# A graph layer on one core: one-hot rows from TensorE products and a relu, and one product per tile in place of two

## The chip, the core and the metric

The kernel runs on one core of one Trainium2 chip. The metric is the device time of one execution in microseconds (us). Times are given as the median of several executions; the profile is of one execution, whose own time is given beside its span.

## What is computed

A layer of a graph network in float32, over N = 6250 nodes with C = 96 features and E = 100,000 edges. Edges are sorted by their target node `dst`. With `BN` for "subtract the mean over all rows, divide by the root of the variance plus 1e-5, scale and shift":

```python
h = relu(layernorm(x))                                   # 6250 x 96
node_feat = BN(relu(h @ W_node + b_node))                # 6250 x 96
edge_feat = BN(relu(edge_attr @ W_edge + b_edge))        # 100000 x 96, edge_attr is 100000 x 4
message = concat([h[src], h[dst], edge_feat], axis=1)    # 100000 x 288
message = BN(relu(message @ W_msg + b_msg))              # 100000 x 96
agg = segment_sum(message, dst, N)                       # 6250 x 96
out = x + agg + node_feat
```

## The kernel before

The message product is split: `h @ W_msg[:96]` and `h @ W_msg[96:192]` are made once for each node and stored in DRAM as `p_table` and `q_table`; the third part acts on the edge features. So a message is relu(p[src] + q[dst] + edge part).

Edges are worked in tiles of 128 and groups of four tiles (512 edges); there are 196 groups, and the last has two tiles. The five engines run programs written by hand, each in its own order, and meet through semaphores. The parts in order of time:

- **Head.** SP loads the nodes; VectorE and ScalarE make the layer norm, TensorE turns the rows and makes `p_table`. POOL at the same time gathers source rows for the first 12 groups directly from `x`. VectorE splits the edge attributes in three bfloat16 parts (`take_off`, L884), SP stores them as 30 rows `x_stack` in DRAM, and VectorE makes from `dst` the place of each edge in its group's window of 96 nodes (`dst_rel`, L907 to L915), with a check that all edges of a group fall in that window (`flag`).
- **Statistics stage.** For all 196 groups TensorE makes relu(edge part), and VectorE takes its mean and variance (L691, L567, L936). The first 12 groups' own rows of `p` are made here too.
- **Message loop** (from L981 on VectorE, `passes(...)` on each engine; `BODY` = 4 groups in one pass of the loop, 49 passes). For each group: SP loads 30 rows of `x_stack` for two groups at once (L423), reads the number of the group's first node (L427) and loads the 96 rows of `q_table` from there (`q_win`, L428). POOL gathers 4 × 128 rows of `p_table` by source node into a ring of 60 groups (L455); it waits only for a free slot. TensorE makes the edge product (L737), turns the bfloat16 one-hots (`hot_b`, L743), adds edge part and `q` part of each tile in PSUM (L759, L761), and sums the messages to the window's nodes with a float32 one-hot (`hot`, L772). ScalarE copies the results of L737 and L743 to SBUF (L605, L607), makes the relu of the messages (L618) and their squares (L622). VectorE builds both one-hots by comparing `dst_rel` with a ramp (L994, L997), adds the gathered rows (L1008), adds messages and squares to `acc` for the mean and variance (L1015), and adds the window to `agg` (L1024).
- **End.** TensorE sums `acc` over the partitions (L813), VectorE makes scale and shift, and twelve blocks of 512 nodes and a rest go through a product with the scale (L825), an addition (L1089) and a store (L441).

The buffers of the loop are two or four groups deep, and the orders overlap: TensorE works at `edges(g + 2)`, `products(g + 1)`, `window_sum(g)`; SP runs up to three groups ahead of `products`. If the check in `flag` fails, a slow general path runs in place of the loop; with these inputs it does not.

```python
wait(sp, pre_summed, g - 3)
base = sp.value_load(base_b[0:1, bass.ds(g, 1)], min_val=0, max_val=N - 1)
sp.dma_start(q_win[0:WIN, j, :], q_table[bass.ds(base, WIN), :]).then_inc(q_in[j], 16)
```

`value_load` reads a number from SBUF into a register of the engine's sequencer and checks its range.

Of the kernel before, what the change touches and what calls it, by code (L numbers as in the profile page):

```python
# [17 lines left out]
N, E, C, EF = 6250, 100000, 96, 4  # L18
P = 128
TILE = P  # L20
# [15 lines left out]
KROWS = len(STACK) * EROWS  # L36
SPLIT_F = EROWS * EP // P
# [18 lines left out]
PACKED = VEC_AT + 7  # L56
# [8 lines left out]
MW = C + 1 + C  # L65


W_GATHER, W_SUMS, W_SCALES, W_DIAG = (8, 4), 5, 9, 2


def graph_layer(nc, x_rows, x_nodes, x_t, src_cols, dst_cols, group_base, edge_rows, packed, w_edge, out_t):
# [5 lines left out]
    x_stack = nc.dram_tensor("x_stack", (KROWS, EP), bf16, kind="Internal").ap()  # L77

    with ExitStack() as ctx:
# [3 lines left out]
        def sem(name):  # L83
# [20 lines left out]
        dst_rel = sb("dst_rel", [P, NG, TPG])  # L104
        base_b = sb("base_b", [P, NG], i32)
        hot = sb("hot", [P, 4, TPG, WIN])
        dst_i = hot[:, :, :, :].bitcast(i32).rearrange("p a t w -> p (a t w)")
        dst_i2 = hot[:, 2:4, :, :].bitcast(i32).rearrange("p a t w -> p (a t w)")
        r_sb = sb("r_sb", [P, 2, 2 * GROUP])
        hot_n = sb("hot_n", [P, 2, GROUP])  # L110
        msg = sb("msg", [P, 2, TPG, MW])
        acc = sb("acc", [P, TPG, MW])
# [6 lines left out]
        hot_b = ln_buf[:, :, :].rearrange("p a f -> p (a f)")[:, 0:2 * TPG * WIN].bitcast(bf16).rearrange(  # L119
            "p (a t w) -> p a t w", a=4, w=WIN)  # L120
        ident_b = sb("ident_b", [P, P], bf16)
        q_win = sb("q_win", [P, 4, C])
# [6 lines left out]
        w3c = sb("w3c", [P, C])  # L129
        we5 = sb("we5", [EROWS, M1])  # L130
        we_split = sb("we_split", [EROWS, 3, M1], bf16)
        we_stack = sb("we_stack", [P, M1], bf16)
        sc = sb("sc", [C, 16])
        t_col = sb("t_col", [C, M1])
        fold = sb("fold", [C, M1])
        s_diag = sb("s_diag", [M1, C])
        bad = sb("bad", [P, 4])
# [7 lines left out]
        pb_b = pb[:, :, :].bitcast(bf16)  # L145
# [13 lines left out]
        rows_cleared = sem("rows_cleared")  # L159
# [44 lines left out]
        turn_built = sem("turn_built")  # L204
        hot_built = sem("hot_built")
        hot_turned = sem("hot_turned")
        hot_kept = sem("hot_kept")
# [19 lines left out]
        gen_square = sem("gen_square")  # L227
# [5 lines left out]
        sums_made = sem("sums_made")  # L233
# [116 lines left out]
        def _(sp):  # L350
# [795 lines left out]
```

## Time and profile before

| | |
|---|---|
| time, median of 3 runs | 1090.58 us (1089.98 to 1091.89) |
| time of the profiled execution | 1093.96 us |
| its span, first to last instruction | 1092.2 us |
| mean granted TensorE clock | 0.889 |
| head, to the first edge product of the statistics stage | 70.5 us |
| first edge product of the message loop | 240.9 us |
| first and last start of a gather from `p_table` | 72.6 and 1068.0 us |

The profile's page gives the busy time of the engines, the span in 40 slices, the chain of work that ended last, the costliest groups of instructions, and the DMAs. Other views give the same by stage, in order of time, or by who waited for whom. PE is TensorE's matmuls, PEld its weight loads, DVE VectorE, ACT ScalarE, POOL GpSimd, SP the engine that only issues DMAs here; L12 is line 12 of the kernel. A float32 matmul shows as two records. A granted clock of 1.00 is 2.4 GHz, and 0.50 is 1.2 GHz.

### The profile page before, as it was taken

Reading aid. Unit: us, or ns where it says so; the run is one execution under the profiler, and the core shown is the slowest. Engines: PE = TensorE matmul, PEld = TensorE weight load, DVE = VectorE, ACT = ScalarE, POOL = GpSimd, SP = SyncE. Lnnn points to the kernel's source line nnn. Section 1 sums busy time; section 2 is a strip of 40 time slices with the busy share of each in tenths; the row PEclk is TensorE's granted clock in tenths of the full one; section 3 lists DMA queues with packets and bytes.
Section 4 is the critical chain, followed back from the end, with each engine's and each line's share of the span. In section 5 each row is a group of like instructions: output and inputs, shape, how many; then the busy total and the mean of one; then the engine's idle time right before and its main releaser. Section 6 shows DMA issues by size and latency. Waiting matters only on the chain.

```text
span 1092.2 us, 23979 instructions
## 1 busy us (share of the span) xinstructions
PE 839.5 (77%) x6383; PEld 726.1 (66%) x6385; DVE 724.6 (66%) x1579; ACT 542.9 (50%) x1012; POOL 826.6 (76%) x786
## 2 busy tenths in 40 slices
PE   2537866639999999999777777777777776877777
PEld 2425622229999999999666666667667666766663
DVE  8678799978898898988444454444444444444445
ACT  3735988836666666666333333333333333333330
POOL 6877777777777777777777777777777777777771
PEclk9867988869999999999888888887898887888889
DMA  8665333352222222222222222222222222222223
GB/s 278 184 225 135 75 85 89 86 150 60 61 57 65 60 58 63 61 59 62 54 49 53 51 52 50 55 49 50 49 56 49 51 54 50 53 49 53 51 45 96
DMA packets 79842, 82.82 MB, mean 76 GB/s; under 512 B 52322, under 2 KB 57074, under 8 KB 79690
## 3 DMA queue, kind: packets, MB, share of 16 engines
q0 software_dynamic: 25024, 38.49, 16.6%
q1 hardware_dynamic: 54148, 42.83, 14.0%
q10 hardware_dynamic: 646, 1.25, 0.4%
q14 instruction: 17, 0.14, 0.0%
q8 instruction: 7, 0.11, 0.0%
HBM read 65.84 MB, written 13.34 MB: 72 GB/s over the span
## 4 chain that ended last, share of the span: by engine, by line
PE 31%; POOL 28%; issue 16%; DMA 11%; DVE 6%; ACT 5%; ACTq 0%; SPq 0%; DVEq 0%; POOLq 0%
POOL ring L455 28%; DMA ring<-p_table,src_idx 8%; PE pc L759 8%; PE pc L761 8%; PE pd L772 6%; DVE edge_st L936 4%; ACT r_sb L567 3%; DMA big_a<-acc 3%; PE pc L666 2%; PE pb L743 2%; PE pa L737 2%; PE pa L691 1%; DVE ln_buf L857 1%; ACT ring L515 1%; DVE ring L878 1%
## 5 line engine op out<-in xcount | busy, mean ns | idle before, releaser
L455 POOL DMA_INDIRECT ring<-p_table,src_idx x734 | 772.9, 1053 | 223.8 <-issue 199.7
L759 PE MATMUL pc<-w3c,r_sb 128*128 128x96 f32 x1564 | 334.0, 298 | 6.3 <-issue 5.9
L761 PE MATMUL pc<-q_win,hot_n 128*128 128x96 f32 x1564 | 322.7, 290 | 0.0
L1008 DVE TENSOR_TENSOR pc<-pc,ring 128x384 f32<-128x384 f32 x196 | 110.8, 565 | 315.3 <-POOLq L482 286.4
L618 ACT ACTIVATE msg<-pc 128x384 f32<-128x384 f32 x196 | 96.4, 492 | 438.3 <-DVE pc L1008 435.5
L772 PE MATMUL pd<-hot,msg 128*97 128x96 f32 x1564 | 192.2, 271 | 136.7 <-ACT msg L618 133.8
L759 PEld LDWEIGHTS pc<-w3c,r_sb 128*128 128x128 f32 x1564 | 262.5, 211 | 13.3 <-issue 10.7
L772 PEld LDWEIGHTS pd<-hot,msg 128*97 128x97 f32 x1564 | 165.8, 181 | 153.7 <-ACT msg L618 111.1
L761 PEld LDWEIGHTS pc<-q_win,hot_n 128*128 128x128 f32 x1564 | 258.6, 208 | 0.0
L1015 DVE TENSOR_TENSOR acc<-acc,msg 128x772 f32<-128x772 f32 x196 | 186.1, 950 | 0.0
L936 DVE BATCH_NORM_STATS2 edge_st<-r_sb 96x512 f32 (+1 forms) x196 | 121.2, 674 | 17.3 <-ACT r_sb L567 15.9
L605 ACT ACTIVATE r_sb<-pa 97x512 f32<-97x512 f32 x196 | 113.3, 578 | 6.4 <-PE pa L737 6.4
L994 DVE TENSOR_TENSOR ln_buf<-dst_rel,pk 128x384 bf16<-128x384 f32 x196 | 108.3, 552 | 5.2 <-issue 5.0
L607 ACT CAST hot_n<-pb 96x512 f32<-96x512 bf16 x196 | 111.4, 569 | 0.3 <-PE pb L743 0.3
L997 DVE TENSOR_TENSOR hot<-dst_rel,pk 128x384 f32<-128x384 f32 x196 | 107.5, 549 | 0.0
L622 ACT ACTIVATE msg<-msg 128x384 f32<-128x384 f32 x196 | 103.2, 526 | 6.2
L743 PEld LDWEIGHTS pb<-ident_b,ln_buf 128*96 128x96 bf16 x782 | 77.5, 140 | 28.1 <-DVE ln_buf L994 8.7
L743 PE MATMUL pb<-ident_b,ln_buf 128*96 128x128 bf16 x782 | 87.6, 242 | 0.3 <-DVE ln_buf L994 0.3
L737 PE MATMUL pa<-xs,we_stack 128*97 128x512 bf16 x196 | 84.5, 431 | 3.9 <-DMA xs<-x_stack 3.9
L455 POOL DMA_INDIRECT ring<-in_x_rows,src_idx x48 | 53.5, 1114 | 18.4 <-issue 14.3
L691 PE MATMUL pa<-xs,we_stack 128*97 128x512 bf16 x98 | 36.0, 455 | 37.9 <-DMA we_stack<-we_split 23.2
L567 ACT ACTIVATE r_sb<-pa 96x1024 f32<-96x1024 f32 x49 | 50.0, 1020 | 16.9 <-DVE edge_st L936 8.4
(110 smaller groups left out, 545.7 us busy)
## 6 DMA issues: line engine op xcount, KB each, us to landing
xs<-x_stack SPq DMA_DIRECT2D x196, 60.0 KB, 1.8
ring<-p_table,src_idx POOLq DMA_INDIRECT x734
q_win<-q_table SPq DMA_DIRECT2D x196, 36.0 KB
x_stack<-ring SPq DMA_DIRECT2D x6, 980.0 KB
ring<-in_x_nodes SPq DMA_DIRECT2D x5, 480.0 KB, 9.8
big_a<-acc SPq DMA_DIRECT2D x1, 2400.0 KB, 12.9
p_table<-ring SPq DMA_DIRECT2D x12, 192.0 KB, 2.5
q_table<-ring SPq DMA_DIRECT2D x12, 192.0 KB
```

The source lines that it names most:

```text
L455: nc.gpsimd.indirect_dma_start(out=ring[:, tile * C:(tile + 1) * C], out_offset=None, in_=table, in_offset=bass.IndirectOffsetOnAxis(ap=id ...
L605: nc.scalar.activation(r_sb[0:M1, j % 2, 0:n], pa[0:M1, j % 2, 0:n], ACT.Relu).then_inc(edge_relu, 1)
L607: nc.scalar.copy(hot_n[0:WIN, j % 2, 0:n], pb_b[0:WIN, j % 2, 0:n]).then_inc(hot_kept, 1)
L743: last = nc.tensor.transpose(pb_b[0:WIN, j % 2, t * TILE:(t + 1) * TILE], hot_b[:, j, t, :], ident_b[:, :])
L759: nc.tensor.matmul(out, r_sb[:, j % 2, t * TILE:(t + 1) * TILE], w3c[:, :], start=True, stop=False)
L761: last = nc.tensor.matmul(out, hot_n[:, j % 2, t * TILE:(t + 1) * TILE], q_win[:, j, :], start=False, stop=True)
L772: last = nc.tensor.matmul(pd[0:M1, j % 2, 0:WIN], msg[:, j % 2, t, 0:M1], hot[:, j, t, :], start=(t == 0), stop=(t == n - 1))
L936: last = V.bn_stats(edge_st[:, bass.ds(u * 2 + half, 1), :].rearrange("c a s -> c (a s)"), r_sb[0:C, k % 2, half * GROUP:half * GROUP + n])
L994: V.tensor_tensor(hot_b[:, j, 0:n, :], rel, ramp[:, :].unsqueeze(1).to_broadcast([P, n, WIN]), ALU.is_equal).then_inc(turn_built, 1)
L997: V.tensor_tensor(hot[:, j, 0:n, :], rel, ramp[:, :].unsqueeze(1).to_broadcast([P, n, WIN]), ALU.is_equal).then_inc(hot_built, 1)
L1008: V.tensor_tensor(pc[:, j % 2, 0:n], pc[:, j % 2, 0:n], ring[:, bass.ds((g % RING) * (TPG * C), n)], ALU.add).then_inc(pre_added, 1)
L1015: V.tensor_tensor(acc[:, 0:n, :], acc[:, 0:n, :], msg[:, j % 2, 0:n, :], ALU.add).then_inc(acc_added, 1)
```

## The change

**One-hots.** In the head, the places of the edges are made in rows (98 × 1024, one number for each edge) rather than columns: relative to the first node of the edge's tile, and relative to that of its group. Each is stored as r, and r² in two bfloat16 parts; these six rows are appended to `x_stack`, which has now 36 rows. With w for a node of the window, 1 − (r − w)² = (1 − w²) + 2wr − r² is linear in (1, r, r²), so a product with fixed coefficients makes it, and its relu is the one-hot. The coefficients for the tile (30 nodes, `TWIN`) are 30 more columns of `we_stack`; those for the group (96 nodes) are `hot_coef`.

**One product for a tile.** The edge product now gives 128 rows: 96 of edge features, one of ones, and 30 of the tile's one-hot; one relu on ScalarE makes them all (`r_sb`). Its partner `w3q` holds the edge weights, the bias, and 30 rows of `q_table`. So L759 and L761 become one product, and SP loads 30 rows for each tile in place of 96 for each group. The group's one-hot is made by four small products into PSUM and a relu on VectorE into `hm`.

**Sums.** `hm` holds for each tile the one-hot, the messages and a column of ones. The window product has 193 columns in place of 96 and gives also messages-times-messages (`gram`); its last column is the sums, its diagonal the sums of squares. The squares on ScalarE, the `acc` addition and the products L813 go. The check is now on windows of 30 nodes for tiles and 96 for groups.

```diff
             sp.wait_ge(stack_stored, 16 * len(STACK))
-            sp.wait_ge(rows_cleared, 1)
+            sp.wait_ge(rel_ready, 1)
+            for k in range(6):
+                sp.dma_start(x_stack[KROWS + k:KROWS + k + 1, :].rearrange("r (p f) -> p (r f)", p=ROWS),
+                             rel_out[:, k, :]).then_inc(rel_stored, 16)
...
+            sp.wait_ge(rel_stored, 16 * 6)
+            sp.wait_ge(main_ready, 1)
             sp.wait_ge(flag_ready, 1)
...
-                            wait(sp, edge_lin, g - 2)
-                            sp.dma_start(xs[0:KROWS, j // 2, :], x_stack[:, bass.ds(g * GROUP, 2 * GROUP)]).then_inc(
+                            wait(sp, hot_lin, g - 2)
+                            sp.dma_start(xs[0:KX, j // 2, :], x_stack[:, bass.ds(g * GROUP, 2 * GROUP)]).then_inc(
                                 x_main[j // 2], 16)
                         wait(sp, pre_summed, g - 3)
-                        base = sp.value_load(base_b[0:1, bass.ds(g, 1)], min_val=0, max_val=N - 1)
-                        sp.dma_start(q_win[0:WIN, j, :], q_table[bass.ds(base, WIN), :]).then_inc(q_in[j], 16)
+                        _, at_node = nc.values_load_multi_w_load_instructions(
+                            bases[0:1, bass.ds(g * TPG + NG, TPG)], [mybir.EngineType.SP], min_val=0, max_val=N - 1)
+                        for t in range(tiles(i, j)):
+                            sp.dma_start(w3q[M1:M1 + TWIN, j, t, :], q_table[bass.ds(at_node[t], TWIN), :]).then_inc(
+                                q_in[j], 16)
...
-                    nc.scalar.activation(r_sb[0:M1, j % 2, 0:n], pa[0:M1, j % 2, 0:n], ACT.Relu).then_inc(edge_relu, 1)
-                    act.wait_ge(hot_turned, g + 1)
-                    nc.scalar.copy(hot_n[0:WIN, j % 2, 0:n], pb_b[0:WIN, j % 2, 0:n]).then_inc(hot_kept, 1)
+                    nc.scalar.activation(r_sb[:, j % 2, 0:n], pa[:, j % 2, 0:n], ACT.Relu).then_inc(edge_relu, 1)
...
-                    wait(act, win_summed, g - 1)
-                    wait(act, acc_added, g - 1)
+                    wait(act, win_summed, g - 3)
...
-                    nc.scalar.square(msg[:, j % 2, 0:n, M1:MW], msg[:, j % 2, 0:n, 0:C]).then_inc(msg_square, 1)
...
-                        last = nc.tensor.transpose(pb_b[0:WIN, j % 2, t * TILE:(t + 1) * TILE], hot_b[:, j, t, :],
-                                                   ident_b[:, :])
+                        at_edge = j % 2 * GROUP + t * TILE
+                        last = nc.tensor.matmul(pb[:, j % 2, t * WIN:(t + 1) * WIN],
+                                                xs[:, j // 2, at_edge:at_edge + TILE], hot_coef[:, :],
+                                                start=True, stop=True)
...
-                    pe.wait_ge(q_in[j], i * 16 + 16)
+                    pe.wait_ge(q_in[j], i * (16 * TPG) + 16 * n)
...
-                        nc.tensor.matmul(out, r_sb[:, j % 2, t * TILE:(t + 1) * TILE], w3c[:, :],
-                                         start=True, stop=False)
-                        last = nc.tensor.matmul(out, hot_n[:, j % 2, t * TILE:(t + 1) * TILE], q_win[:, j, :],
-                                                start=False, stop=True)
+                        last = nc.tensor.matmul(pc[:, j % 2, t * C:(t + 1) * C], r_sb[:, j % 2, t * TILE:(t + 1) * TILE],
+                                                w3q[:, j, t, :], start=True, stop=True)
...
-                        last = nc.tensor.matmul(pd[0:M1, j % 2, 0:WIN], msg[:, j % 2, t, 0:M1], hot[:, j, t, :],
+                        last = nc.tensor.matmul(pd[0:M1, j % 2, 0:HW], hm[:, j, t, WIN:HW], hm[:, j, t, :],
...
-                    V.tensor_tensor(hot_b[:, j, 0:n, :], rel, ramp[:, :].unsqueeze(1).to_broadcast([P, n, WIN]),
-                                    ALU.is_equal).then_inc(turn_built, 1)
-                    V.tensor_tensor(hot[:, j, 0:n, :], rel, ramp[:, :].unsqueeze(1).to_broadcast([P, n, WIN]),
-                                    ALU.is_equal).then_inc(hot_built, 1)
+                    V.tensor_scalar(hm[:, j, 0:n, 0:WIN], pb[:, j % 2, 0:n * WIN].rearrange("p (t w) -> p t w", w=WIN),
+                                    0.0, None, ALU.max).then_inc(hot_built, 1)
...
-                    V.tensor_tensor(acc[:, 0:n, :], acc[:, 0:n, :], msg[:, j % 2, 0:n, :],
-                                    ALU.add).then_inc(acc_added, 1)
+                    V.tensor_tensor(gram[:, :], gram[:, :], pd[0:M1, j % 2, WIN:HW], ALU.add).then_inc(gram_added, 1)
...
-            V.tensor_tensor(w3c[C:M1, :], pd[C:M1, 0, 0:C], bm_row[C:M1, :], ALU.add).then_inc(main_ready, 1)
+            V.tensor_tensor(w3q[C:M1, :, :, :].rearrange("p j t c -> p (j t) c"),
+                            pd[C:M1, 0, 0:C].unsqueeze(1).to_broadcast([1, BODY * TPG, C]),
+                            bm_row[C:M1, :].unsqueeze(1).to_broadcast([1, BODY * TPG, C]),
+                            ALU.add).then_inc(main_ready, 1)
...
-            link(V.tensor_scalar(sc[:, 0:2], pd[0:C, 0, 0:2], 1.0 / E, None, ALU.mult))
+            link(V.tensor_tensor(diag[:, :], gram[0:C, 0:C], ident[0:C, 0:C], ALU.mult))
+            link(V.tensor_reduce(sc[:, 1:2], diag[:, :], AX, ALU.add))
+            V.tensor_scalar(sc[:, 0:1], gram[0:C, C:M1], 1.0 / E, None, ALU.mult)
+            link(V.tensor_scalar(sc[:, 1:2], sc[:, 1:2], 1.0 / E, None, ALU.mult))
```

The order of SP's instructions for one group in the message loop. Before (`ISA` is a register instruction of the sequencer, the first with the wait, the next two the range check, the last the DMA's address):

```order
L427 ISA [waits pre_summed]
L427 TENSOR_LOAD base_b
L427 ISA x2
L428 ISA
L428 DMA q_win<-q_table 96x96
```

With the change:

```order
L435 ISA [waits pre_summed]
L435 TENSOR_LOAD bases
L435 ISA x8
L438 ISA
L438 DMA w3q<-q_table 30x96
L438 ISA
L438 DMA w3q<-q_table 30x96
L438 ISA
L438 DMA w3q<-q_table 30x96
L438 ISA
L438 DMA w3q<-q_table 30x96
```

One load now fills four registers, four range checks follow it, and four DMAs stand where one stood.

VectorE in the head, between the split of the edge weights and the second subtraction of `take_off`. Before:

```order
L901 CAST we_split<-we 5x97 [waits dve_step]
L907 TENSOR_TENSOR dst_rel<-hot,base_b 128x784 [waits dst_in]
L911 TENSOR_SCALAR msg<-dst_rel 128x784 [waits dve_step]
L912 TENSOR_TENSOR msg<-msg 128x784 [waits dve_step]
L913 TENSOR_REDUCE bad<-msg 128x1 [waits dve_step]
L914 COPY bad<-msg 32x1
L915 TENSOR_SCALAR bad<-bad 128x2 [waits dve_step]
L917 MEMSET msg 128x4 x2
L919 MEMSET r_sb 128x2048
L920 MEMSET hot_n 128x1024
L922 TENSOR_REDUCE flag<-pd 1x1 [waits bad_counted]
L884 TENSOR_TENSOR big_b<-big_b,ring 128x3920 [waits split_step]
```

With the change (the ten rows from L908 to L921 stand there twice, once for tiles and once for groups):

```order
L908 TENSOR_TENSOR r_sb<-w3q,row_base 98x1024 [waits dst_in]
L912 CAST hm<-r_sb 98x1024 [waits dve_step]
L913 TENSOR_TENSOR r_sb<-r_sb 98x1024
L914 CAST hm<-r_sb 98x1024 [waits dve_step]
L915 TENSOR_TENSOR hm<-r_sb,hm 98x1024 [waits dve_step]
L917 TENSOR_SCALAR r_sb<-r_sb 98x1024 [waits dve_step]
L918 TENSOR_TENSOR r_sb<-r_sb 98x1024 [waits dve_step]
L919 TENSOR_REDUCE bad<-r_sb 98x1 [waits dve_step]
L920 TENSOR_REDUCE bad<-r_sb 97x1
L921 TENSOR_SCALAR bad<-bad 128x2 [waits dve_step]
```

The subtraction of `take_off` stands behind all of them, with one memset of `w3q` (128x1536) between.

## Rows read from the trace of the kernel before

**Rows 1.** The page, parts 1 and 2, and waits: engine, line waited for: us, times, longest
```profile
PE 839.5 (77%) x6383; PEld 726.1 (66%) x6385; DVE 724.6 (66%) x1579; ACT 542.9 (50%) x1012; POOL 826.6 (76%) x786
...
GB/s 278 184 225 135 75 85 89 86 150 60 61 57 65 60 58 63 61 59 62 54 49 53 51 52 50 55 49 50 49 56 49 51 54 50 53 49 53 51 45 96
...
DVE pc L1008 <- POOLq L482: 286.4, 100, 5.2
```

**Rows 2.** Busy time by stage, us: all engines, granted clock, DMA share, GB/s
```profile
72.60:226.00 153.40, 110.43 (x483) 60.31 (x482) 138.03 (x288) 120.21 (x161) 116.01 (x123) 0.87 0.38 94
255.00:505.00 250.00, 250.00 (x2469) 242.11 (x2468) 225.29 (x448) 167.60 (x341) 198.20 (x170) 1.00 0.27 61
520.00:1060.00 540.00, 401.45 (x2913) 360.80 (x2911) 261.33 (x530) 198.67 (x404) 417.74 (x402) 0.85 0.23 51
```

**Rows 3.** The line of the gathers: ns min/median/max, first and last start
```profile
L455 POOL DMA_INDIRECT ring<-p_table,src_idx x734: 940/944/1510, 72.6 to 1068.0; - x184
```

**Rows 4.** The gathers alone by the same stages: POOL busy (count), clock, DMA, GB/s
```profile
72.60:226.00 153.40, 116.01 (x123) 0.87 0.38 94
255.00:505.00 250.00, 198.20 (x170) 1.00 0.27 61
520.00:1060.00 540.00, 417.74 (x402) 0.85 0.23 51
```

**Rows 5.** Timeline from 702 us, POOL and VectorE: start us, us, engine line operation
```profile
702.38 0.94 POOL L455 DMA_INDIRECT ring<-p_table,src_idx  x1 [0.30 <-issue]
702.71 0.57 DVE L1008 TENSOR_TENSOR pc<-pc,ring 128x384 f32<-128x384 f32 x1 [2.84 <-POOLq L482]
703.19 0.95 DVE L1015 TENSOR_TENSOR acc<-acc,msg 128x772 f32<-128x772 f32 x1
703.63 1.32 POOL L455 DMA_INDIRECT ring<-p_table,src_idx  x1 [0.30 <-issue]
```

**Rows 6.** Timeline from 300 us, TensorE's weight loads in one group
```profile
300.13 0.13 PEld L737 LDWEIGHTS pa<-xs,we_stack 128*97 128x97 bf16 x1
...
301.04 0.30 PEld L759 LDWEIGHTS pc<-w3c,r_sb 128*128 128x128 f32 x2
...
301.27 0.30 PEld L761 LDWEIGHTS pc<-q_win,hot_n 128*128 128x128 f32 x2
...
302.38 0.77 PEld L772 LDWEIGHTS pd<-hot,msg 128*97 128x97 f32 x8
...
303.07 0.13 PEld L737 LDWEIGHTS pa<-xs,we_stack 128*97 128x97 bf16 x1
```

**Rows 7.** Waits of SP's queue
```profile
SPq L427 <- PE pc L761: 409.7, 192, 6.4
```

**Rows 8.** Lines 427, 428 and 423 on SP: ns min/median/max, first and last start
```profile
L427 SPq FUSED_REGOPS  x384: 37/152/161, 232.2 to 1047.9; - x192
L427 SPq TENSOR_LOAD <-base_b x196: 268/428/1922, 230.2 to 1047.6; - x196
L427 SPq SEQ_ASSERT  x196: 18/18/18, 232.4 to 1048.1; - x196
...
L428 SPq FUSED_REGOPS  x196: 37/37/48, 232.4 to 1048.2; - x196
L428 SPq MOVE q_win<-q_table x196: 29/29/45, 232.5 to 1048.2; - x196
L428 SPq DMA_DIRECT2D q_win<-q_table x196: 317/317/902, 232.6 to 1048.3; - x196
...
L423 SPq DMA_DIRECT2D xs<-x_stack x98: 373/373/2358, 229.0 to 1038.8; - x98
L423 SPq FUSED_REGOPS  x94: 42/50/51, 243.0 to 1018.0; - x94
```

**Rows 9.** Timeline, SP from 255 us
```profile
256.43 0.32 SPq L428 DMA_DIRECT2D q_win<-q_table  x1
256.93 0.32 SPq L410 DMA_DIRECT2D res<-in_x_t  x1
```

**Rows 10.** Timeline of the head, VectorE
```profile
42.26 0.95 DVE L907 TENSOR_TENSOR dst_rel<-hot,base_b 128x784 f32<-128x784 int32 x1
43.24 0.57 DVE L911 TENSOR_SCALAR msg<-dst_rel 128x784 f32<-128x784 f32 x1
43.85 0.98 DVE L912 TENSOR_TENSOR msg<-msg 128x784 f32<-128x784 f32 x1
...
49.22 0.08 DVE L922 TENSOR_REDUCE flag<-pd 1x1 int32<-1x2 f32 x1
50.98 4.24 DVE L884 TENSOR_TENSOR big_b<-big_b,ring 128x3920 f32<-128x3920 f32 x1 [1.68 <-ACT ring L515]
```

**Rows 11.** Timeline before the message loop, SP and VectorE
```profile
229.01 1.15 SPq L423 DMA_DIRECT2D xs<-x_stack  x1
...
240.23 0.26 DVE L971 TENSOR_TENSOR w3c<-pd,pk 1x96 f32<-1x96 f32 x1 [3.63 <-DMA big_a<-acc]
```

**Rows 12.** Timeline of the end, VectorE
```profile
1075.17 0.15 DVE L1072 TENSOR_SCALAR sc<-pd 96x2 f32<-96x2 f32 x1 [1.35 <-PE pd L813]
```

More of the change, by code:

```diff
@@ L690, in p1_unit @@
                 for half in range(2):
-                    last = nc.tensor.matmul((pa, pb)[k % 2][0:M1, half, :], we_stack[:, :],
+                    last = nc.tensor.matmul((pa, pb)[k % 2][0:M1, half, :], we_stack[:, 0:M1],
                                             xs[:, k, half * GROUP:(half + 1) * GROUP], start=True, stop=True)
@@ L839, in _ @@
             V = nc.vector
[L841 removed]
+            V.memset(zeros[:, :], 0.0).then_inc(zeroed, 1)
             V.memset(ones[:, :], 1.0)
@@ L845, in _ @@
             V.memset(xs[:, :, :], 0.0)
-            V.memset(w3c[:, :], 0.0)
-            V.memset(q_win[:, :, :], 0.0)
+            V.memset(hot_coef[:, :], 0.0)
+            V.memset(gram[:, :], 0.0)
+            V.memset(hot_n[:, :, :], 0.0)
             V.memset(bad[:, :], 0.0)
@@ L911, in _ @@
-            link(V.tensor_scalar(far, rel, -(WIN - 1) / 2.0, None, ALU.add))
-            link(V.tensor_tensor(far, far, far, ALU.mult))
-            V.tensor_reduce(bad[:, 0:1], far[:, 0:full], AX, ALU.max)
-            link(V.tensor_copy(bad[0:LAST_ROWS, 1:2], far[0:LAST_ROWS, full:full + 1]))
-            V.tensor_scalar(bad[:, 2:4], bad[:, 0:2], (WIN / 2.0) ** 2, None, ALU.is_gt).then_inc(bad_ready, 1)
-            for k in range(2):
-                V.memset(msg[:, k, :, C:M1], 1.0)
-            V.memset(r_sb[:, :, :], 0.0)
@@ L921, in _ @@
+            last.then_inc(bad_ready, 1)
+            dve.sem_inc(rel_ready, 1)
+            V.memset(w3q[:, :, :, :], 0.0)
             dve.wait_ge(bad_counted, 1)
-            V.tensor_reduce(flag[0:1, 0:1], pd[0:1, 0, 0:2], AX, ALU.max).then_inc(flag_ready, 1)
+            V.tensor_reduce(flag[0:1, 0:1], pd[0:1, 0, 0:4], AX, ALU.max).then_inc(flag_ready, 1)
             take_off(1)
@@ L1025, in add_sums @@
                                     ALU.add).then_inc(win_added, 1)
-                for j in range(3):
+                for j in range(2):
                     build_hot(0, j)
@@ L1120 @@
         packed[:C, VEC_AT + k] = w[name]
+    for at, rel, n in ((HOT_AT, REL_T, TWIN), (HOT_AT + TWIN, REL_G, WIN)):
+        w_at = _np.arange(n)
+        low = (1 - w_at * w_at) % 64
+        packed[0, at:at + n] = 1 - w_at * w_at - low
+        packed[EROWS, at:at + n] = low
+        packed[rel, at:at + n] = 2 * w_at
+        packed[rel + 1:rel + 3, at:at + n] = -1.0
     w_edge = _np.zeros((EROWS, M1), _np.float32)
```

198 lines of the change are left out of this document (105 added, 93 removed).

## Prediction

> **What bounds the kernel now.** I read the page's busy shares, then the gathers by stage, then the waits. The reader should see in [rows 1] that no engine is full over the whole span, that POOL's indirect gathers are the costliest group and that VectorE waits 286.4 us for POOL's `gathered` counts. The stages in [rows 2] differ: from 255 to 505 us TensorE is busy all of the time at its 2.4 GHz level (granted clock 1.00) and works off the backlog of gathered groups; from 520 to 1060 us it is busy 74% at 0.85 and waits. POOL never stops: its gathers run from 72.6 to 1068.0 us [rows 3], and the queue behind them is what ends last. So today's end is 734 gathers long, and what SP, TensorE and VectorE need for a group of four gathers is hidden as long as it keeps the mean below (1068 − 241) / 196 = 4.2 us [rows 3, 11]. That number decides this case.
>
> **The gathers get faster.** In [rows 4] a gather takes 943 ns busy in 123 cases while the statistics stage runs (VectorE is 90% busy there too, on one-input work), 1,166 ns while the message loop runs at full speed, and 1,039 ns in the last stage; with the 0.30 us between two of them [rows 5] the periods are 1.25, 1.47 and 1.34 us. [rows 5] show the cause: the gather that starts at 702.38 takes 0.94 us beside L1008, which reads PSUM and SBUF; the one at 703.63 takes 1.32 us beside L1015, 0.95 us with both inputs in SBUF. The change takes L1015 away and both L994 and L997 (two SBUF inputs, 0.55 us each), and puts in their place a relu from PSUM and an addition with one PSUM input. What is left with two SBUF inputs in the loop is L978, once in four groups. So the gathers go to 1.24 us: 734 × 1.24 = 910 us in place of 995, from about 75.5 us (3 us later, for the two-input passes in the head, below). POOL would then issue its last gather at 986, and with the 24.2 us from the last gather to the end [rows 3] (1,092.2 − 1,068.0), less 1 us (below), the span would be 1,009 us. That is the floor.
> The Trainium skill (SBUF — State Buffer, Who interferes with whom) says that a Vector instruction with two SBUF inputs contends only with GpSimd work that reads SBUF, and it infers that descriptor generation is not such work. By that rule the gathers would stay where they are and the floor would be 1,092 us; [rows 4, 5] speak against it.
>
> **TensorE, VectorE and ScalarE.** In the full stage TensorE needs 2.94 us for a group, from one L737 at 300.13 to the next at 303.07 [rows 6]. Of these, 16 f32 product records take 0.11 us each (0.23 from 301.04 to 301.27 for two), and the change drops the 8 of L761; four small transposes become four small products. The window product goes from 96 to 193 columns: its 8 records take 0.69 us, 302.38 to 303.07, and twice the columns is at most twice that, so +0.7 against −0.9 us. So about 2.8 us, some 3.2 at a granted clock of 0.85: below SP's number, so priced at nothing. VectorE loses 0.55 + 0.55 + 0.95 us and gains some 0.55 + 0.25; ScalarE loses L607 and L622. Both were covered and stay so.
>
> **SP, the part that I think decides.** Today SP issues one DMA of 96 rows for a group and then waits: 409.7 us for products in all [rows 7]. The change makes it load four numbers, check each, and issue four DMAs of 30 rows, and the products of a group wait for all four. The register rows [rows 8] and two DMAs that start back to back, 256.43 and 256.93 [rows 9], give the price: 0.50 us = 0.317 + 0.037 + 0.029 and three gaps of 0.04. For a group, when SP waits for nothing:
> - wait and address, 0.05 + 0.04 = 0.09;
> - the load, 0.27 to 0.43 for one number, mean 0.35, + 0.04 = 0.39;
> - four pairs of check and assert, 4 × (0.152 + 0.018 + 0.08) = 1.00;
> - four DMAs at 0.50 = 2.01;
> - half an `xs` load, (0.050 + 0.029 + 0.373 + 0.12) / 2 = 0.29; a quarter of a `res` load, 0.13; counters and branches, some 0.1.
> That is 4.0 us before the load of four numbers is priced. No row shows such a load: it costs nothing more at the least, and three more loads, 3 × 0.27 = 0.81, at the most. I take 0.35, nearer to one instruction than to four, since one address is computed. The check is also uncertain: its 0.152 stands beside 0.037 to 0.05 for other register rows of two or three operations. If the 0.11 difference is a wait for the loaded number, only the first check pays it, and the group is 0.33 cheaper. So SP's pace is 3.7 at the least, 4.8 at the most; 4.35 is my value.
>
> **The head.** L907 to L915 (42.26 to 46.1) and the memsets behind them, up to 49.22, go [rows 10]. In their place VectorE makes 2 × 10 passes, most over 98 × 1024: by [rows 10] a two-input pass of 784 takes 0.95 to 0.98 us, so 1.23 for 1024; a one-input pass 0.57, so 0.72. Twice (four at 1.23, three at 0.72, one reduction at 1.2, a third of one, a small one) is 18.4 us, plus 1.4 for the memset of `w3q` (three quarters of the 2048 columns that are cleared today). The subtraction L884 that follows then starts at 62.5 in place of 50.98: +11.5 us, and it is on the path, since `we_stack` and the last `x_stack` piece come behind it. SP then puts six stores of 0.2 MB on its queue before the first `xs` load; at the 185 to 225 GB/s of the head [rows 1] that is 5 to 6 us, some 4 of it not covered. The statistics stage and what follows move by 15 us. POOL doesn't feel it: it needs the flag at 72.6 [rows 3], and the flag moves from 49.22 [rows 10] to about 62.
> Before the loop, L971 becomes 1 × 1536 in place of 1 × 96 (+1.4 us), and SP, which today fills its buffers from 229.01 on [rows 11], now waits for it. SP enters the loop at 240.23 + 15 + 1.7 + 0.6 = 257.5 us.
>
> **The sum.** 257.5 + 196 × 4.35 (852.6) = 1,110. The last window lands 2 us later (as the `xs` loads do), the last group's products, addition, relu and window product take 2, and from L1072 at 1075.17 to the end it is 17.0 us today [rows 12]. Ahead of it the sums L813 and the wait for them give way to the addition to `gram` and four small VectorE steps, 1.5 us together, where today 2.4 pass. Span 1,110 + 4 + 1.5 + 17.0 = 1,132.5; today's is 1,092.2, so +40.3. The profiled execution took 1,093.96 in all, 3.4 above the median 1,090.58; the forecast in the median's terms is 1,131.
>
> **The rivals.**
> 1. *SP is cheaper than I price it* (checks 0.33 less, the four-number load free). Pace 3.7 to 4.1: 257.5 + 196 × 3.85 + 22.5 = 1,035 span, with the gathers' floor at 1,009 just below. This is **faster**, and it decides as soon as SP's pace is under 4.14 us, where 257.5 + 196 × pace + 22.5 is today's span. For it: the register rows of other kinds are short. Against: every check in the rows took 0.152. Chance 0.26, 1,008 to 1,083.
> 2. *Each number pays for its own load.* The group takes 4.0 + 0.81 = 4.8 us, the span 257.5 + 941 + 22.5 = 1,221. For it: even one number takes 0.27 to 0.43, far more than any other register row. The Trainium skill (Runtime: NRT & Kernel Launch) puts such loads at about 200 ns for each register even in bulk; by that estimate the pace is 4.6 and the span 1,182. No row here shows it. Chance 0.25, 1,170 to 1,240.
> 3. *TensorE falls to its 1.2 GHz level* because it waits for SP between short bursts. At half the clock 2.8 us become 5.6 and the span 257 + 1,098 + 23 = 1,378. Against: at 74% busy the clock was 0.85 [rows 2]. Chance 0.03.
> 4. *The gathers don't get faster*, and SP is cheap: the end stays with POOL, about 1,092 to 1,095. Chance 0.03.
> My case, a pace of 4.2 to 4.6 with SP ahead of all, has 0.39 and its own range is 1,103 to 1,180; 0.04 is left for a pace that lands on today's time.
>
> **How the numbers follow.** A run can tell about 0.2% from nothing. Faster: rival 1 and a little of rival 4, 0.28. Same: 0.04. Slower: 0.68. The range must take in rival 1's middle and most of rival 2: 1,018 to 1,215 leaves out the bottom of rival 1 (0.05), the top of rival 2 (0.08) and rival 3.
>
> **What would show it.** Right: SP's own waits for products nearly vanish from 409.7 us; the starts of the last `w3q` DMA of two groups lie 4.2 to 4.6 us apart throughout; TensorE waits for DMAs into `w3q`; POOL's gathers take 0.94 us in every stage and end near 990, long before the span; no two stages of the loop differ, as 255 to 505 and 520 to 1060 do now. Wrong: SP still waits and VectorE waits for POOL to the end (rival 1 at its floor), gathers still at 1.04 us or more (rival 4), or TensorE full at a clock near 0.5 (rival 3). The first loop instruction should start near 258 us, the first edge statistics near 87 in place of 72.75.

## The result, and the profile after

The changed kernel takes 1,120.8 us, the kernel before 1,090.8 on the same chip (medians of four executions each): the ratio is 1.026, 95% interval 1.024 to 1.029. The change makes the kernel **2.6% slower**. The forecast was 1,131 with a range of 1,018 to 1,215. Of the changed kernel's four executions three took 1,117.4 to 1,121.5 us; the fourth took 1,359.9 with a mean granted clock of 1.00 where the others had 0.87, is left out of the ratio, and is not explained. The profiled execution took 1,120.07 us, its span is 1,118.3.

The page of the changed kernel: busy time, and the shares of the chain that ended last, by engine and by line.
```profile
PE 781.5 (70%) x4800; PEld 635.8 (57%) x4800; DVE 544.2 (49%) x1401; ACT 369.7 (33%) x620; POOL 750.8 (67%) x786
...
SPq 54%; issue 21%; DVE 10%; PE 7%; ACT 5%; DMA 3%; ACTq 0%; DVEq 0%
SPq L438 28%; SPq L435 20%; DVE edge_st L941 4%; SPq L431 3%; ACT r_sb L577 3%; SPq L416 2%; PE pc L670 2%; DMA big_a<-zeros 1%; DMA xs<-x_stack 1%; PE pa L695 1%; PE pc L762 1%; PE pd L773 1%; DVE ln_buf L856 1%; DVE ring L877 1%; SPq L273
```
Against [rows 1] every compute engine has less to do, and more than half of the chain is now SP's queue: L438 issues the `w3q` loads, L435 waits, loads the four numbers and checks them.

The gathers, their line and then alone by stage (columns as in [rows 3, 4]; the last gather starts at 991.7, inside the third stage).
```profile
L466 POOL DMA_INDIRECT ring<-p_table,src_idx x734: 940/944/1500, 75.6 to 991.7; - x184
```
```profile
72.60:226.00 153.40, 115.92 (x124) 0.85 0.40 100
255.00:505.00 250.00, 189.03 (x201) 0.88 0.29 62
520.00:1060.00 540.00, 357.33 (x379) 0.88 0.26 57
```
The gathers run at 0.94 us in all stages, where [rows 4] had 1.17 and 1.04 in the loop. They end 76 us earlier than in [rows 3], and yet the span is 26 us longer. TensorE is no longer full in the first part of the loop: 185.16 us busy from 255 to 505 us, in the view of all engines, where [rows 2] have 250.00.

SP's lines: ns min/median/max, first and last start.
```profile
L435 SPq FUSED_REGOPS  x972: 66/147/162, 254.3 to 1091.3; - x195
L435 SPq SEQ_ASSERT  x784: 18/18/24, 254.5 to 1091.5; - x196
L435 SPq TENSOR_LOAD <-bases x196: 458/464/557, 253.7 to 1089.9; - x196
...
L438 SPq FUSED_REGOPS  x782: 37/42/48, 255.3 to 1092.1; - x196
L438 SPq MOVE w3q<-q_table x782: 29/29/42, 255.4 to 1092.2; - x196
L438 SPq DMA_DIRECT2D w3q<-q_table x782: 327/328/1177, 255.5 to 1092.3; - x196
```
196 loads lie between 253.7 and 1,089.9 us, 4.29 us from one to the next. SP's queue has no wait at all between 260 and 1,100 us; its last one of note stands ahead of the loop, and TensorE waits instead. From the waits of SP's queue, then of all engines (engine, line waited for: us, times, longest):
```profile
SPq L421 <- DVE w3q L979: 15.9, 1, 15.9
```
```profile
PE pa L741 <- DMA xs<-x_stack: 204.1, 91, 8.2
```
The 409.7 us for products of [rows 7] are gone, and so are the 286.4 us of VectorE for POOL [rows 1].

### The profile page after: what moved, and what is told of

Read it like the earlier page. It is cut to its first block, busy times and chain, and to the rows that moved or that the text cites. A ratio compares the mean times of both kernels' runs of the same rounds, so it can differ in the third digit from the quotient of the medians.

```text
span 1118.3 us, 22745 instructions
## 1 busy us (share of the span) xinstructions
PE 781.5 (70%) x4800; PEld 635.8 (57%) x4800; DVE 544.2 (49%) x1401; ACT 369.7 (33%) x620; POOL 750.8 (67%) x786
## 4 chain that ended last, share of the span: by engine, by line
SPq 54%; issue 21%; DVE 10%; PE 7%; ACT 5%; DMA 3%; ACTq 0%; DVEq 0%
SPq L438 28%; SPq L435 20%; DVE edge_st L941 4%; SPq L431 3%; ACT r_sb L577 3%; SPq L416 2%; PE pc L670 2%; DMA big_a<-zeros 1%; DMA xs<-x_stack 1%; PE pa L695 1%; PE pc L762 1%; PE pd L773 1%; DVE ln_buf L856 1%; DVE ring L877 1%; SPq L273 1%
## 5 line engine op out<-in xcount | busy, mean ns | idle before, releaser
L466 POOL DMA_INDIRECT ring<-p_table,src_idx x734 | 693.5, 945 | 223.8 <-issue 197.6
L773 PE MATMUL pd<-hm 128*97 128x193 f32 x1564 | 341.4, 368 | 0.0
L773 PEld LDWEIGHTS pd<-hm 128*97 128x97 f32 x1564 | 281.0, 191 | 9.8
L762 PE MATMUL pc<-w3q,r_sb 128*128 128x96 f32 x1564 | 245.7, 307 | 13.9 <-DMA w3q<-q_table 7.7
L762 PEld LDWEIGHTS pc<-w3q,r_sb 128*128 128x128 f32 x1564 | 218.2, 216 | 20.3 <-issue 9.7
L741 PE MATMUL pa<-xs,we_stack 128*128 128x512 bf16 x196 | 83.4, 426 | 204.3 <-DMA xs<-x_stack 204.1
L615 ACT ACTIVATE r_sb<-pa 128x512 f32<-128x512 f32 x196 | 116.8, 596 | 326.6 <-PE pa L741 323.8
L1004 DVE TENSOR_SCALAR hm<-pb 128x384 f32<-128x384 f32 x196 | 109.1, 557 | 222.6 <-PE pb L747 195.5
L625 ACT ACTIVATE hm<-pc 128x384 f32<-128x384 f32 x196 | 96.3, 491 | 312.2 <-DVE pc L1015 304.2
L1015 DVE TENSOR_TENSOR pc<-pc,ring 128x384 f32<-128x384 f32 x196 | 110.8, 565 | 97.9 <-PE pc L762 91.5
L466 POOL DMA_INDIRECT ring<-in_x_rows,src_idx x48 | 57.1, 1189 | 17.8 <-issue 14.3
L695 PE MATMUL pa<-xs,we_stack 128*97 128x512 bf16 x98 | 35.4, 448 | 37.5 <-DMA we_stack<-we_split 22.5
L577 ACT ACTIVATE r_sb<-pa 96x1024 f32<-96x1024 f32 x49 | 50.0, 1020 | 18.6 <-PE pa L695 9.6
```

Of the source, the lines that this page charges most:

```text
L466: nc.gpsimd.indirect_dma_start(out=ring[:, tile * C:(tile + 1) * C], out_offset=None, in_=table, in_offset=bass.IndirectOffsetOnAxis(ap=id ...
L577: nc.scalar.activation(r_sb[0:C, k % 2, :], (pa, pb)[k % 2][0:C, :, :].rearrange("c a b -> c (a b)"), ACT.Relu).then_inc(p1_relu, 1)
L615: nc.scalar.activation(r_sb[:, j % 2, 0:n], pa[:, j % 2, 0:n], ACT.Relu).then_inc(edge_relu, 1)
L741: nc.tensor.matmul(pa[:, j % 2, 0:n * TILE], we_stack[:, :], xs[:, j // 2, j % 2 * GROUP:j % 2 * GROUP + n * TILE], start=True, stop=True) ...
L762: last = nc.tensor.matmul(pc[:, j % 2, t * C:(t + 1) * C], r_sb[:, j % 2, t * TILE:(t + 1) * TILE], w3q[:, j, t, :], start=True, stop=True)
L773: last = nc.tensor.matmul(pd[0:M1, j % 2, 0:HW], hm[:, j, t, WIN:HW], hm[:, j, t, :], start=(t == 0), stop=(t == n - 1))
```

## The experiments

The median of the kernel before was 1,093.1 to 1,094.2 us in these comparisons and 1,090.8 in the first, so a difference of 2 or 3 us between two comparisons says nothing. Two theories were set against each other: **A**, SP's own instructions set the pace; **B**, the four small DMAs themselves do.

**e1: no range checks.** The checks of the four numbers go.
```
-    bases[0:1, bass.ds(g * TPG + NG, TPG)], [mybir.EngineType.SP], min_val=0, max_val=N - 1)
+    bases[0:1, bass.ds(g * TPG + NG, TPG)], [mybir.EngineType.SP], min_val=0, max_val=N - 1,
+    skip_runtime_bounds_check_because="each is the first node of a tile, checked by flag")
```


> Theory A (SP's own instructions set the pace of the loop, 4.28 us for a group, of which the four range checks are 4 x 0.26 = 1.03 us): the pace falls to 3.25 us if nothing else holds, so the gathers set the end; last gather at 992 us as with the change, span 1,010 to 1,018 us, time near 1,015 us, SP waits for products again. Rival B (the pace is set by the DMAs themselves, their queue or their landing, not by SP's instructions): the checks cost nothing, time stays at 1,120 us.

Measured 1,018.8 us, ratio 0.932 (0.931 to 0.934). The same DMAs, loads and products, and 102 us less than the changed kernel. SP waits for products again, and VectorE for gathers (waits of SP's queue, then of all engines):
```profile
SPq L435 <- PE pc L763: 64.0, 38, 5.9
```
```profile
DVE pc L1016 <- POOLq L494: 168.3, 56, 5.6
```
A holds, and the floor is POOL's.

**e2: one more load.** A one-number load with its check is put ahead of the four-number load, and nothing uses it.
```
+    sp.value_load(bases[0:1, bass.ds(g, 1)], min_val=0, max_val=N - 1)
     _, at_node = nc.values_load_multi_w_load_instructions(
```


> One more load of one number with its check for each group, unused. Theory A: 0.3 to 0.5 us for the load, 0.26 for the check, 0.1 for the address, so +0.7 to +0.85 us for each of 196 groups: time 1,257 to 1,287 us. Rival B: 1,120 us.

Measured 1,233.5 us (two runs), ratio 1.128 (1.125 to 1.132): 113 us, or 0.58 us a group, more than the changed kernel's 1,120.8, and less than expected. The two loads, the new one first:
```profile
L435 SPq TENSOR_LOAD <-bases x196: 438/443/542, 259.4 to 1204.9; - x196
...
L436 SPq TENSOR_LOAD <-bases x196: 298/302/318, 260.2 to 1205.7; - x196
```
The load of *one* number takes 443 ns and that of *four*, right behind it, 302. So the count of numbers costs nothing that shows. What stands around the load does: in e3, below, the loads of two numbers take 0.640 us on SP and 0.663 on ScalarE (medians).

**e3: the issue split.** ScalarE's queue loads, checks and issues tiles 2 and 3 of a group, SP tiles 0 and 1; the products wait for both.
```
-    for t in range(tiles(i, j)):
+    for t in range(2):
...
+    act.dma_start(w3q[M1:M1 + TWIN, j, 2 + t, :], q_table[bass.ds(at_node[t], TWIN), :]).then_inc(q_act[j], 16)
...
-    pe.wait_ge(q_in[j], i * (16 * TPG) + 16 * n)
+    pe.wait_ge(q_in[j], i * 32 + 32)
+    pe.wait_ge(q_act[j], i * 32 + 32)
```


> ScalarE's sequencer loads, checks and issues for two of the four tiles of a group, SP for the other two. Theory A: SP needs 2.7 us for a group and ScalarE about 3.6 (1.1 us of work, 2.1 for its half, waits), both below the gathers' 5.0 us; time near 1,015 us, last gather at 992. Rival B: the number and size of DMAs are the same and they share the DMA engines: 1,120 us.

Measured 1,018.2 us, ratio 0.932 (0.930 to 0.933).

**e7: split, and no checks.**

> Both together. Theory A: the gathers already set the end of each one alone, so nothing is gained over them: 1,010 to 1,018 us. Rival B: 1,120 us. If the end is not with the gathers but with ScalarE's or SP's rest, this one is faster than either alone.

Measured 1,019.1 us, ratio 0.932 (0.930 to 0.933). Either cure alone reaches the floor, and both together win nothing more. A holds: e1 has every transfer of the changed kernel, and e3 has them too, issued from two queues.

That settles the new bound. The second question is why the gathers got faster, and what they cost the kernel before. **C**: VectorE's instructions with two inputs in SBUF stretch them. **D**: they don't.

**e4, e5, e6: the kernel before, without the addition, without the one-hots, without either.** In e5 and e6 L994 is replaced in the same way as L997 below, from the fifth group on.
```
-    V.tensor_tensor(acc[:, 0:n, :], acc[:, 0:n, :], msg[:, j % 2, 0:n, :], ALU.add).then_inc(acc_added, 1)
+    dve.sem_inc(acc_added, 1)
```
```
-    V.tensor_tensor(hot[:, j, 0:n, :], rel, ramp[:, :].unsqueeze(1).to_broadcast([P, n, WIN]),
-                    ALU.is_equal).then_inc(hot_built, 1)
+    V.memset(hot[:, j, 0, 0:1], 0.0).then_inc(hot_built, 1)
```


> The kernel before, without the addition of L1015 (VectorE, 128x512, both inputs in SBUF), so that the message sums are left out and the scale and shift that come of them are wrong. Theory C (a VectorE instruction that reads two inputs from SBUF stretches the gathers beside it; 0.385 to 0.40 us a group of the kernel before is such stretch, and the addition is the larger share of it): about 33 us less than the kernel before, near 1,060; gathers' mean between 0.97 and 0.99 us where the stage rows of the kernel before had 1.04 to 1.17. Rival D (the skill's rule: such instructions do not contend with descriptor generation; the stretch comes of something else, VectorE's general load or the transfers): no change, near 1,093, gathers' mean as before.

> The kernel before, with the one-hots of L994 and L997 built for the first four groups alone (a one-column memset in their place behind that), so that tables of other groups are used and the output is wrong by that. Theory C: about 37 us less than the kernel before, near 1,055, if both one-hot builds stretch the gathers; near 1,072 if only L997 does, since the slope of the gathers' time on the overlap with L994 is about zero in the trace of before. Rival D: no change, near 1,093, though VectorE has some 1.3 us a group less to do.

> The kernel before with both edits: neither the addition of L1015 nor the one-hot builds behind the fourth group. Message sums are left out and the one-hots are stale. Theory C: the gathers run at their floor of 1.247 us each, 734 of them, and the time is 1,018 to 1,025. Rival D: near 1,093.

(The addition is 128x772, as [rows 5] show, not 128x512 as e4's text has it.)

Measured: e4 1,039.2 us, ratio 0.951 (0.950 to 0.953); e6 1,014.9, ratio 0.929 (0.928 to 0.931). e5: 1,088.6 to 1,091.0 in seven executions and 1,054.5 in an eighth, whose mean granted clock was 0.73 where the others had 0.89. The gathers' line in the kernel before, e4, e5 and e6 (count, then busy us and mean ns of one):
```profile
L455 POOL DMA_INDIRECT ring<-p_table,src_idx x734 | 772.9, 1053 | 223.8 <-issue 199.7 <-DMA ring<-p_table,src_idx 14.0 <-DVE pc L1008 10.1
L455 POOL DMA_INDIRECT ring<-p_table,src_idx x734 | 719.1, 980 | 223.7 <-issue 197.8 <-DMA ring<-p_table,src_idx 24.1 <-DVE pc L1008 1.8
L455 POOL DMA_INDIRECT ring<-p_table,src_idx x734 | 769.2, 1048 | 223.7 <-issue 201.8 <-DMA ring<-p_table,src_idx 22.0
L455 POOL DMA_INDIRECT ring<-p_table,src_idx x734 | 693.0, 944 | 223.7 <-issue 200.5 <-DMA ring<-p_table,src_idx 20.1 <-DVE pc L1015 3.0
```
With neither, the kernel before reaches the floor, so VectorE's instructions do stretch the gathers, and D falls. But the shares are not sums of parts: without the addition 54 us go, not 33; without the one-hots 3.3 us in the seven executions, not 37; without both 78. The traces say why. Put down the time of each gather over 0.944 us to the VectorE instruction that is under way at its start: in the kernel before the addition has 70.3 us (193 gathers), L997 9.3 (71), L994 0.6 (2). In e4 L997 has 14.2 and L994 12.2 (145 gathers): with the addition gone, the one-hots lie across more starts. In e5 the addition has 76.2 (193 gathers again). The sums, 80.0, 26.2, 76.3 and 0.1 us, differ by what the times differ by, to 2 us. e5's eighth execution lies where C expected e5; it has no trace, and what e5 saves in that other rhythm stays open. The next four kernels ask what the price is of.

**e8: the addition's twin in the changed kernel.** To e3 comes, in each group, a VectorE maximum of 128x772, both inputs in SBUF, whose result nothing uses.
```
+    scratch = hot_n[:, :, :].rearrange("p a f -> p (a f)")[:, 0:772]
+    V.tensor_tensor(scratch, scratch, scratch, ALU.max).then_inc(spent, 1)
```


> The changed kernel with its issue split over two sequencers (as e3), and in each group one VectorE maximum of 128x772 more, both inputs and the output in SBUF, whose result nothing uses. VectorE has room for it (busy about half of the span). Theory C: the gathers are stretched again, mean about 0.99 us, and the time is some 30 to 40 us above e3, near 1,050. Rival D: as e3, near 1,018.

Measured 1,090.8 us (ten executions, 1,082 to 1,100), ratio 0.997 (0.994 to 0.999): 72.6 us above e3, twice what was expected, from 196 instructions of 0.95 us on an engine that is half idle. The timeline shows what happens (start us, us, engine, line, operation):
```profile
698.28 0.94 POOL L468 DMA_INDIRECT ring<-p_table,src_idx  x1 [0.30 <-issue]
699.17 0.95 DVE L1044 TENSOR_TENSOR hot_n<-hot_n 128x772 f32<-128x772 f32 x1
699.53 1.41 POOL L468 DMA_INDIRECT ring<-p_table,src_idx  x1 [0.30 <-issue]
```
The maximum starts during one gather, which still takes 0.94 us, and ends at 700.12, 0.59 us after the next has started; that one takes 1.41, or 0.47 us too long. The gather is not slowed in proportion. It is longer by what is left, at its start, of the VectorE instruction under way, less some 0.12 us.

**e9, e10, e11: one input, half the length, bfloat16.** The same place in the group, with other instructions.
```
+    V.tensor_scalar(scratch, scratch, 0.0, None, ALU.max).then_inc(spent, 1)
+    wait(dve, spent, 2 * g + 1)
+    V.tensor_scalar(scratch, scratch, 0.0, None, ALU.max).then_inc(spent, 1)
```
That is e9, with e8's 128x772 `scratch`. e10 keeps e8's line with `scratch` cut to 386 columns, and e11 with 1,544 columns of the same buffer as bfloat16.

> The control of e8: in place of the maximum of 128x772 with two inputs in SBUF, two maxima with a constant in each group, 128x772 too, each with one input and its output in SBUF, so that VectorE moves the same output twice and is busy for about as long. Theory C (it is the second SBUF input that stretches the gathers): near 1,018, gathers' mean 0.945 us as in e3. Rival E (any long VectorE instruction on SBUF stretches them): 1,060 or more, gathers' mean over 1.0 us. Rival F (e8's price came from VectorE's time in its chain and not from the gathers): between the two, with the gathers unchanged.

> As e8, with a maximum of 128x386: half the length, some 0.5 us. Theory C with a price by the length of the overlap: half of e8's 72.6 us above e3, near 1,054, or less where part of it falls into the 0.3 us between two gathers. With a price by the number of instructions: the whole, near 1,090.

> As e8, with operands in bfloat16, 128x1544: the same bytes as e8's 128x772 in fp32. The trace of before had L994, whose output is bfloat16, at no stretch, and L997, with an fp32 output, at 0.4 us per us of overlap. If the type of the output decides: near e3, 1,018. If two inputs in SBUF decide, whatever their type: 1,080 to 1,130 by how long it lasts.

Measured: e9 1,034.6 us, ratio 0.946 (0.944 to 0.947), so 16.5 above e3; e10 1,034.9, ratio 0.945 (0.944 to 0.947), 16.7 above; e11 1,096.2, ratio 1.003 (1.002 to 1.005), 78 above. e9 lies between the values expected by C and by E, and e10 far below the half. F, VectorE's own chain, falls: the gathers' time over 0.944 us is 14.3 us in e9, 16.3 in e10 and 77.6 in e8 against 1.0 in e3, so the gathers alone account for the prices. One rule explains both. In the timelines, first e10, then e9:
```profile
705.86 0.55 DVE L1044 TENSOR_TENSOR hot_n<-hot_n 128x386 f32<-128x386 f32 x1
706.25 0.97 POOL L468 DMA_INDIRECT ring<-p_table,src_idx  x1 [0.31 <-issue]
```
```profile
709.20 0.55 DVE L1044 TENSOR_SCALAR hot_n<-hot_n 128x772 f32<-128x772 f32 x1
709.48 1.09 POOL L468 DMA_INDIRECT ring<-p_table,src_idx  x1 [0.30 <-issue]
709.79 0.56 DVE L1046 TENSOR_SCALAR hot_n<-hot_n 128x772 f32<-128x772 f32 x1
```
In e10 0.16 us of the maximum are left when the gather starts, and it loses 0.03; in e9 0.27 are left and it loses 0.15. So half the length costs a quarter: in e10 95 gathers are held, by 0.15 us on average, and in e8 190 by 0.40. And an instruction with one input in SBUF and its output there holds a gather up too; it costs less here since it is over in 0.55 us and the second of the pair starts when the gather is under way. Not every such instruction does: in the statistics stage of the kernel before 107 gathers start with a batch_norm_stats (L936, one input in SBUF, an output of 6 columns) under way and 0.47 us of it left on average, and none takes over 0.95. The maximum of e9 moves its 772 columns in 0.55 us where the one with two inputs takes 0.95; whether that faster form or the wide output in SBUF makes the difference was not tried. The bfloat16 maximum of the same bytes lasts as long and costs as much, so the type isn't what counts:
```profile
702.20 0.95 DVE L1046 TENSOR_TENSOR hot_n<-hot_n 128x1544 bf16<-128x1544 bf16 x1
702.50 1.46 POOL L468 DMA_INDIRECT ring<-p_table,src_idx  x1 [0.30 <-issue]
```
The Trainium skill (SBUF — State Buffer, Who interferes with whom) has VectorE and GpSimd share a port pair as an exclusive lock, and the shape of these rows agrees with a lock. In the same section the Trainium skill infers that a two-input instruction leaves descriptor generation alone; the gathers are issued by GpSimd, and e8, e10 and e11, 72.6, 16.7 and 78 us above e3, speak against that.

**e12: the same work in another place.** If the price is of the moment, the kernel before needs no change of its work, only of its order. The addition goes ahead of L1008, right behind the wait for the gathered rows; nothing is left out (`add_msg` is the addition of the group before).
```
     dve.wait_ge(pre_summed, g + 1)
     dve.wait_ge(gathered, g + 1)
+    if before is not None:
+        add_msg(*before)
     V.tensor_tensor(pc[:, j % 2, 0:n], pc[:, j % 2, 0:n],
```


> The kernel before with two of its VectorE instructions in the other order, and nothing left out: in each group the addition of the message sums (L1015, 128x772, 0.95 us) stands right behind the wait for the gathered rows and ahead of L1008, where it stood behind L1008. In the traces a gather is longer by what is left, at its start, of a VectorE instruction on SBUF, less some 0.1 us, and a gather that has started is not longer. The addition of the kernel before started 0.7 to 0.9 us behind a gather's start, and so was in flight when the next one began, 1.25 us behind it; moved ahead it would start some 0.25 to 0.3 us behind a gather's start and be done at 1.25. Theory C in this form (the price is of the place, not of the work): 1,020 to 1,050, the gathers' mean between 0.945 and 0.985, where what is left comes of the one-hots L994 and L997. If the price is of the work (so many us of two-input instructions anywhere beside gathers): as before, near 1,093.

Measured 1,070.6 us, ratio 0.979 (0.977 to 0.981): 22.7 us faster than the kernel before by the order of two instructions, though the expected 1,020 to 1,050 was missed.
```profile
699.69 0.94 POOL L455 DMA_INDIRECT ring<-p_table,src_idx  x1 [0.30 <-issue]
699.88 0.96 DVE L1017 TENSOR_TENSOR acc<-acc,msg 128x772 f32<-128x772 f32 x1 [2.55 <-POOLq L482]
...
700.94 0.94 POOL L455 DMA_INDIRECT ring<-p_table,src_idx  x1 [0.30 <-issue]
...
701.85 0.55 DVE L997 TENSOR_TENSOR hot<-dst_rel,pk 128x384 f32<-128x384 f32 x1
...
702.19 1.03 POOL L455 DMA_INDIRECT ring<-p_table,src_idx  x1 [0.30 <-issue]
```
The addition (L1017 here) now ends at 700.84, ahead of the next start at 700.94, and costs neither gather anything, where the same instruction cost 0.38 us in [rows 5]. But the one-hots behind it were pushed across the start at 702.19, and from 255 to 505 us VectorE never waits for gathers, so that the edit fixes nothing there. e12's gathers alone, by stage:
```profile
255.00:505.00 250.00, 198.19 (x171) 1.00 0.27 61
520.00:1000.00 480.00, 366.95 (x372) 0.87 0.25 54
```
The first stage is as in [rows 4]; the gain is in the last: 0.986 us a gather in place of 1.039. Put down as above, the addition's part from 505 us on falls from 37.7 to 1.9 us and that of the one-hots rises from 3.1 to 18.3; before 505 us the addition still has 22.6 and the one-hots 15.9. That is where the expected 1,020 to 1,050 was missed. e12 also shows what L994, the one-hot with a bfloat16 output, does by itself:
```profile
402.79 0.56 DVE L994 TENSOR_TENSOR ln_buf<-dst_rel,pk 128x384 bf16<-128x384 f32 x1 [0.37 <-issue]
402.91 1.25 POOL L455 DMA_INDIRECT ring<-p_table,src_idx  x1 [0.30 <-issue]
403.26 0.55 DVE L997 TENSOR_TENSOR hot<-dst_rel,pk 128x384 f32<-128x384 f32 x1
```
0.44 us of L994 are left at the gather's start and the gather loses 0.31: it goes by L994's end (403.35), not by L997's.

Over the whole loops the rule can be counted. In the kernel before, from 240 us on, 266 gathers take, or should take by the rule, over 0.964 us, and all 266 lie within 0.02 us of it, with 0.125 us in place of 0.12. In the eight traces with such instructions (before, e4, e5, e8 to e12) it is 1,380 of 1,434. Of the 54 others 34 are gathers that lose nothing beside a VectorE instruction that began at most 0.04 us ahead of them, and eleven are gathers of e9 that take 0.05 to 0.24 us longer with none of the pair under way at their start: in that kernel a gather that has started can be held up too, and why is not shown.

## Why the prediction was right

**What bounds the kernel now, and the threshold.** Right. The forecast turned on whether SP stays under 4.2 us a group. SP takes 4.29 and the kernel is slower; e1 takes the four checks from it, 1.05 us, and e3 half of the issue, and both are 6.8% faster than before.

**The gathers.** Right in size: 0.94 us in each stage, first at 75.6 (forecast 75.5), last at 991.7 (986). The floor of 1,009 us of span is 1,015.4 in e1; a gather's period is 1.25 us and not the 1.24 of the sum. The cause was named too narrowly. It put the stretch down to two inputs in SBUF, over the overlap; e9 shows that one input can do it, and e8 with e10 that what counts is what is left of the instruction when a gather starts. The three instructions were in the right list all the same, but in the kernel before the addition holds up 193 gathers and L994 two; L994 counts only once the others are moved or gone (e4, e12).

**TensorE, VectorE, ScalarE.** Not the bound, as forecast. TensorE waits 204.1 us for DMAs, but the prediction said for those into `w3q`: it is the `xs` loads that come last, since SP issues each of them behind the four DMAs of the group before. Waits for `w3q` are 7.7 us.

**SP's pace.** 4.35 was forecast, 4.29 measured; the parts:

| part, us a group | forecast | measured |
|---|---|---|
| load of four numbers, with its gap | 0.39 + 0.35 | 0.50 |
| four checks | 1.00 | 1.05 |
| four DMAs | 2.01 | 2.11 |
| the rest (wait, `xs`, `res`, counters) | 0.61 | 0.63 |

The first three are means of 195 groups, each from the start of its first row to that of the next part's; the first DMA of a group takes some 0.05 us more than the row's 0.328. The rest is what is missing to 4.29. The term that failed is the load: three more numbers were given 0.35 us and cost nothing (e2), while the load itself is 0.11 longer than the mean of 0.35 taken from [rows 8]. That the forecast fell on the slower side is in part luck: with the three numbers free, as e2 has them, the prediction's own sum is 257.5 + 196 × 4.0 + 22.5 = 1,064 us, faster than before. What it then had too small, 0.28 us a group over the load, the checks, the DMAs and the rest, took the place of the 0.35. Rival 2 falls with it: four loads' worth would have been 0.81 more. By the 200 ns for each register that the Trainium skill (Runtime: NRT & Kernel Launch, Instruction fetch mechanics) gives, four would take 0.8 us; the rows have 0.464, and 0.302 behind another load. But the Trainium skill (the same page, Terms) means by it registers loaded from HBM, and these numbers are in SBUF. Of rival 1's two conditions the free load of four numbers holds, and the other, that only the first check costs 0.152, falls: the four of a group take 152, 152, 147 and 147 ns (medians).

**The head.** Too high. SP entered the loop at 253.3 us, not 257.5, and the first edge statistics came at 82.5 us, 9.8 later than the 72.7 of before, where 87 was forecast. The passes of the head had been put at +11.5 us and moved the subtraction L883 by 8.0:
```profile
58.98 0.09 DVE L927 TENSOR_REDUCE flag<-pd 1x1 int32<-1x4 f32 x1
59.00 4.23 DVE L883 TENSOR_TENSOR big_b<-big_b,ring 128x3920 f32<-128x3920 f32 x1
```
and the six stores take 3.72 us of SP's queue:
```profile
70.70 3.72 SPq L383 DMA_DIRECT2D x_stack<-hm  x6
74.47 0.83 SPq L391 DMA_DIRECT2D xs<-x_stack  x1
```

**The sum.** Span 1,118.3 for 1,132.5, 14.2 us less: the start of the loop 4.2, the pace 196 × 0.062 = 12.1, and against them 2.1 more behind the loop (24.6 for 22.5). Of the rivals the first (1,035, from a cheap SP) came nearest: SP without the checks does lead to the gathers' floor, as e1 shows, but with them SP is not that cheap. With the loop's start and end as measured, the changed kernel takes as long as the one before at (1,092.2 − 253.3 − 24.6) / 196 = 4.15 us a group: its loss hangs on 0.13 us a group.

## What to carry to other kernels

When a loop's pace is set by gathers or another long queue, count what the sequencers issue in an iteration as one counts matmuls: here a range check is 0.26 us, a DMA 0.51 to 0.56, a load of one, two or four registers 0.27 to 0.66 with no dependence on their number that shows, and a second queue that takes half of it, or doing without the checks, turned a loss of 2.6% into a gain of 6.8%. Beside gathers issued by GpSimd, look not at how busy VectorE is but at which of its instructions from SBUF to SBUF is under way when a gather starts: keep those short, read from PSUM (in the changed kernel 0.3 us left of L1015 or L1004 cost nothing), or start them just behind a gather's start. A wait for the gathers themselves fixes that place, for good or ill.

## What the hardware showed that was not expected

- The price of one VectorE instruction beside the gathers goes from 0 to more than 0.5 us with its start: 0.95 us long and begun 0.19 us behind a gather's start it costs nothing (e12, 699.88), begun 0.89 us behind it costs 0.47 (e8, 699.17). In the kernel before the addition starts 0.81 us behind a gather's start in [rows 5], and 0.73 to 0.87 behind one in eight cases of ten, near the worst place. From 505 us on the wait of L1008 for the gathers puts it there; before that VectorE does not wait for gathers, and what holds the place is not shown.
- Two such costs are not a sum: 54 us and 3.3 us for the parts, 78 for both (e4, e5, e6), since an instruction that goes moves the others against the gathers. The one execution of e5 at 1,054.5 us, with TensorE's clock lower, is not explained; that another rhythm moved the addition off the starts would fit, and was not tried.
- A load of four registers takes 464 ns behind a DMA issue and 302 behind another load and its check (e2), a load of one 268 at the least in [rows 8] and 443 in e2, and a load of two 640 when a second queue loads too (e3). Why is open.
